# A GNN layer on one NeuronCore: in steps with picks, ScalarE normalises three of a block's four tiles and VectorE one

## The reference

```python
h = relu(layernorm(x))                 # x: 50000 x 128, no scale or shift
xx = resmlp(h, MLP 0)                  # for all nodes
xs, xp, xd = resmlp(h, MLP 1, 2, 3)[dst]       # for 12500 edges
s = xx + segment_sum((rbf @ w_rs) * xs, src)
p, d = segment sums of (rbf @ w_rp) * xp * attr3 and of (rbf @ w_rd) * xd * attr5
y = s + inner products of the halves of p @ w_pp and of d @ w_pd
out = x + resmlp(y, MLP 4)

def resmlp(x, w1, b1, w2, b2, wout):
    h = x + silu(silu(x) @ w1 + b1) @ w2 + b2
    return silu(h) @ wout
```

## Time and profile before

| | |
|---|---|
| median of 3 runs | 1262.18 us (1259.76 to 1266.66) |
| the profiled execution | 1264.56 us |
| its span, first to last instruction | 1262.7 us |
| mean granted TensorE clock | 0.963 |
| busy: PE, ACT, DVE, POOL | 1135.0, 758.2, 660.6, 456.9 us |
| HBM read and written | 93.01 and 96.30 MB |

### The profile page before, as it was taken

One profiled execution on the slowest core, in us unless ns is written; L12 is line 12 of the kernel. 1 busy time (PEld: TensorE's weight loads), 2 busy tenths in 40 slices (PEclk: granted clock), 3 DMA queues, 4 the chain that ended last, 5 costly groups with the idle time before them and its releaser, 6 DMA issues.

```text
span 1262.7 us, 23295 instructions
## 1 busy us (share of the span) xinstructions
PE 1135.0 (90%) x6835; PEld 766.0 (61%) x6835; DVE 660.6 (52%) x2466; ACT 758.2 (60%) x1425; POOL 456.9 (36%) x423
## 2 busy tenths in 40 slices
PE   2778998797989856999999999999977999999998
PEld 1555665474656533666666666666744666666665
DVE  9866876695778303565556555655541222222222
ACT  2357878656877833555655565556524666666665
POOL 3055666015565531456555655565340000000000
PEclk9889999898999978999999999999988999999999
DMA  7166667735766430233333333333435888788876
GB/s 223 67 213 199 224 213 224 253 129 162 232 217 211 165 89 11 46 57 46 54 55 57 47 54 55 55 49 52 83 55 170 250 263 263 247 266 258 256 257 206
DMA packets 162765, 190.56 MB, mean 151 GB/s; under 512 B 57956, under 2 KB 82444, under 8 KB 162413
## 3 DMA queue, kind: packets, MB, share of 16 engines
q1 hardware_dynamic: 124636, 144.39, 38.4%
q0 software_dynamic: 23920, 19.29, 9.7%
q10 hardware_dynamic: 14112, 25.70, 5.3%
HBM read 93.01 MB, written 96.30 MB: 150 GB/s over the span
## 4 chain that ended last, share of the span: by engine, by line
PE 77%; DVE 11%; issue 7%; DMA 2%; ACT 1%; another core or an unknown queue 1%; SPq 0%; POOL 0%; ACTq 0%; POOLq 0%; DVEq 0%
PE bank L976 7%; PE quad L964 7%; PE bank L1489 5%; PE quad L968 5%; PE bank L1499 5%; PE bank L811 4%; PE quad L795 4%; PE bank L1563 4%; PE bank L1531 3%; DVE onehot L589 3%; PE bank L1564 3%; PE quad L804 3%; PE quad L956 3%; PE quad L780 2%; DVE stat L484 2%
## 5 line engine op out<-in xcount | busy, mean ns | idle before, releaser
L1164 POOL DMA_INDIRECT node_sums<-rowout,row_i x98 | 155.0, 1582 | 199.6 <-ACT rowout L1426 177.1
L900 DVE TENSOR_TENSOR rowout<-bank,xin 128x512 f32<-128x512 f32 x98 | 67.8, 692 | 242.0 <-PE bank L976 242.0
L811 PEld LDWEIGHTS bank<-wo_sb,s 128*128 128x128 f32 x784 | 102.8, 194 | 64.9 <-issue 64.9
L431 POOL DMA_INDIRECT edges_by_src<-pay,rank_i x98 | 96.2, 981 | 111.5 <-DVE rank_i L619 50.6
L431 POOL DMA_INDIRECT edges_by_low<-pay,rank_i x98 | 96.6, 986 | 99.3 <-DVE rank_i L619 42.2
L976 PEld LDWEIGHTS bank<-wo_sb,s 128*128 128x128 f32 x784 | 102.8, 191 | 47.8 <-issue 47.8
L1197 DVE SCALAR_TENSOR_TENSOR h<-bank,b_sb,hT 128x512 f32<-128x512 f32 (+1 forms) x75 | 55.5, 740 | 122.2 <-PE bank L1499 122.2
L484 DVE BATCH_NORM_STATS2 stat<-xin 128x6 f32<-128x128 f32 x392 | 105.4, 284 | 21.9 <-DMA xin<-in_x_dram 21.9
L811 PE MATMUL bank<-wo_sb,s 128*128 128x128 f32 x784 | 106.0, 279 | 11.0 <-issue 9.0
L72 POOL DMA_INDIRECT yin<-node_h,er x98 | 94.9, 968 | 53.8 <-issue 29.3
L709 ACT ACTIVATE xn<-xin,nbias,rnorm 128x128 f32<-128x128 f32 x210 | 101.8, 492 | 14.3 <-DVE nbias L535 14.3
(11 more groups left out here) (193 smaller groups left out, 2376.1 us busy)
## 6 DMA issues: line engine op xcount, KB each, us to landing
xin<-in_x_dram SPq DMA_DIRECT2D x196, 256.0 KB, 3.9
node_h<-xn SPq DMA_DIRECT2D x98, 256.0 KB
node_sums<-rowout SPq DMA_DIRECT2D x98, 256.0 KB
yin<-node_sums SPq DMA_DIRECT2D x98, 256.0 KB, 4.0
out_dram<-rowout ACTq DMA_DIRECT2D x98, 256.0 KB, 3.8
border_sums_by_tile<-border_sums SPq DMA_DIRECT2D x24, 256.0 KB, 2.1
pay<-edges_by_low POOLq DMA_DIRECT2D x1, 2058.0 KB, 10.7
edges_by_low<-pay,rank_i POOLq DMA_INDIRECT x98
```

The source lines that it names most:

```text
L431: nc.gpsimd.indirect_dma_start(out=ps.dram, out_offset=bass.IndirectOffsetOnAxis(ap=rank_i[:, t:t + 1], axis=0), in_=pay[:, t, :], in_offs ...
L811: last = nc.tensor.matmul(BANK_O[:, j * P:(j + 1) * P], s3[:, (k - 3) % 3, j * P:(j + 1) * P], wo_sb[:, m, :], start=True, stop=True)
L1164: nc.gpsimd.indirect_dma_start(out=ysum, out_offset=bass.IndirectOffsetOnAxis(ap=row_i[:, t % 2, j:j + 1], axis=0), in_=urow[:, t % 2, j, ...
```

## The change

In steps with picks `by_scalar` gives 3 in place of 2: tiles 1, 2 and 3 are ACT's (tiles 1 and 2 ahead of L733, tile 3 behind it), and DVE's subtraction and rectification take tile 0 alone. The steps at the start of a pass (4) and the steps without picks (2) stay. No semaphore is added or taken away; the waits for `nrm_v`, `nrm_a` and the old store of the slot move with the tiles.

```diff
             def by_scalar(b):
 
                 k = max(b - 1, 0)
-                return TB if any(ps.onehots <= k <= ps.onehots + T // OH for ps in passes) else TB // 2
+                if any(ps.onehots <= k <= ps.onehots + T // OH for ps in passes):
+                    return TB
+                return 3 if picks_at(k) else TB // 2
```

## The result

| | before | after |
|---|---|---|
| median of 15 runs each, one after the other | 1261.82 us (1258.41 to 1266.66) | 1267.36 us (1264.62 to 1269.64) |
| ratio | | 1.0043, 95% interval 1.0032 to 1.0054 |
| span of the profiled execution | 1262.7 us | 1267.8 us |

The kernel is 5.5 us slower, 0.43%, against 5.6 us forecast. The interval of the ratio leaves out 1, so the loss is real, though small.

What follows compares the result with a forecast made beforehand. PE was taken to set the pace, waiting for ACT's last normalisation after a disturbance. 4.3 us from 11 disturbed B steps plus 1.3 from 15 undisturbed made 5.6 us, 0.44%, so 1268 us; range 1256 to 1275 (8 in 10).

Steps and rivals of the forecast that it cites:

- disturbance: About every second or third step: ACT idles 1.5 to 2.1 us, matmul completion reaching it late, and PE runs dry.
- A steps: 28 steps with a chunk's first four picks, 3.84 us each; ACT's waiting there covers the extra 0.39 us: cost nothing.
- A steps past 3.84 us: Sign in the profile after that the prediction would be wrong: A steps growing longer than 3.84 us.
- B steps without a disturbance: 15 steps with a chunk's last three picks: 12 lose 0.06 us, three 0.20, sum 1.3 us; 3.11 for 3.05 us.
- The three with a lag: Three undisturbed B steps, step 32 first, where ACT came in slightly late: 0.20 us late each.
- B steps with a disturbance: 13 steps with a chunk's last three picks: 11 listed blocks lose 0.39 us each, 4.3 us; two lose nothing.
- The next stage's loads near 460: SP's first loads of the next stage were to start near 460 in place of 454.20, the first stage's loss staying lost.
- Free steps: Steps without picks, still two and two: way back after a disturbance no longer than now; ACT's lateness goes into 2.11 us waiting.
- DVE's relief: DVE's subtraction and rectification 0.28 us less a step, 15.7 us busy time in all; taken as worth nothing on the path.
- the rival with the other sign: Rival that DVE was the bound, each step it sets gaining 0.28 us: faster, 1255.2 us with 45 such steps; chance 0.13.
- ACT becomes the bound in every B step: Rival: ACT's list 3.28 us against PE's 3.05, all 28 B steps cost 0.39: 10.9 us, 1273.1; chance 0.17.
- The disturbances hide it: Rival: late completions come at fixed times, so only undisturbed B steps' 1.3 us stays: 1263.5 us; chance 0.20.

Runs made afterwards that it cites:

- VectorE's part alone: Kernel before, with VectorE normalising one tile in steps with picks, ScalarE still two and tile 1 left out: 1267.25 against 1265.76 us, ratio 1.0007.
- ScalarE's part alone: Kernel before, with ScalarE also normalising tile 1 into an unread tile in steps with picks, VectorE still two: 1270.53 against 1265.76 us, ratio 1.0039.
- the A steps alone: Changed kernel with three tiles on ScalarE in A steps only, against the kernel before: 1266.17 against 1265.76 us, ratio 1.0002.
- the chip without disturbances: Changed kernel, unaltered, against the kernel before on a chip where the latter takes 1194 us: 1195.86 against 1194.00 us, ratio 1.0015.
- the opposite change: Kernel before with ScalarE one tile, VectorE three in B and free steps, two and two in A: 1261.83 against 1264.70 us, ratio 0.9979.

## Why the prediction was right

- *PE sets the pace, ACT's last normalisation is what it waits for behind a disturbance, and in no step of the two stretches VectorE.* Shown: VectorE's part alone 1.0007, ScalarE's part alone 1.0039 of 1.0043. (The 28 A and 28 B steps that the prediction counts are those of the two whole passes; the two stretches of the earlier trace rows hold fewer.)
- *A steps cost nothing.* Shown by the A steps alone (1.0002), and by the 0.46 us of wait that went. The prediction also named A steps past 3.84 us as a sign of being wrong, and two came out so (11 and 63, above). They are longer by a disturbance that fell there and not by the added operation, which stands ahead of the idle time; what such a shift is worth by itself no run tells.
- *B steps without a disturbance cost 0.06 us.* They cost 0.05: 3.10 for 3.05 in all traces. The three with a lag, put at 0.20, take 3.10 as well, where they took 3.05 to 3.07. On the chip without disturbances 28 x 0.05 is 1.4 us, and measured by the ratio were 1.8 (0.4 to 3.2). In its traces the step behind a B step is some 0.03 us longer too: 0.66 us for the 8 B steps between blocks 18 and 38 and 0.97 for the 12 between 58 and 87, so 0.08 for each.
- *B steps with a disturbance cost 0.39 us.* True of block 26, 0.38 us by its idle time. As a list of eleven blocks it is not what happened: once steps are longer the disturbances fall otherwise. In the profile after the B steps 20 and 30 are 1.18 and 1.10 us longer and the free steps 18 and 28 0.57 and 0.54 shorter. From block 18 to 38 the sum is 1.97 us, where the prediction's terms for them (four blocks at 0.39, four B steps at 0.06 to 0.20) give 1.9; from 63 to 87 it is 3.7 against 2.5; and from block 4 to 18 the profile after took 2.0 us less. By the medians the part that needs disturbances is 5.5 less 1.8, 3.7 us, against 4.3 forecast.
- *The next stage's loads near 460.* They came at 457.76: the first stage of that pair lost 3.6 us. The 5.5 us is a difference of medians.
- *Free steps keep their length.* Wrong in the single step: some are half a us shorter, which the longer B steps more than make up.
- *DVE's relief and the rival with the other sign.* This rival fell by VectorE's part alone (1.0007), as did "ACT becomes the bound in every B step": its 0.39 us in each would be 10.9 us, and the chip without disturbances shows 0.05, or 0.08 with the step behind.
- *The disturbances hide it.* This rival also fell for the change (ACT's idle time stayed near 40 us, and the loss is four times its 1.3 us), but when the work was taken away, in the opposite change, most of the gain did not come: 2.9 us of up to 9.8. So the full price of 0.39 us behind each disturbance held for adding work and not for taking it away.

That the sum came out within 0.1 us of the measured one is partly luck: one execution differs from the next by more, and the positions of the disturbances were taken from a single one. The prediction held that about 0.5% can be told from no change; with 15 executions of each kernel it was 0.11% either way.

What stays open: why the matmuls' completion reaches ScalarE late on one chip while GpSimd scatters, and not on two others, and whether the spacing of the scatters matters there.

## What to carry to other kernels

When work moves between engines, find for each kind of step which engine's last instruction releases the bound one, and by how much; a move costs the instruction's full share of a back-to-back row (0.39 us here, not its recorded 0.49) where that gap is zero, the overrun where it is small, and nothing where the engine waits. Do it per kind of step, not by busy shares: here VectorE was at 76% and ScalarE at 78%, both under PE, and in these stretches only one of them was waited for. The releaser named by a view is checked against the block or tile that the waiting instruction needs.

## What the runs showed of the hardware

- The same kernel took 1262 to 1266 us where it was first measured and on the chip of the first eight runs, and 1194 on two others. Most of the difference is in the first stage: up to the last block's transposes 443.1 us and 384.2, which is 58.9 of the 71.3 us between the spans (1262.7 and 1191.4). From 98 to 199 us ACT has ten idle times of 0.7 to 2.1 us in the one trace, and none in the other.
- Two of these idle times, looked at in the trace's semaphore records, end when several of PE's signals come at once, though its matmuls are recorded as done at different times before. In the kernel before, the output matmuls, the transposes and the first matmul ended by their records at 147.43, 147.86 and 148.72 us, and their semaphores were counted up at 148.87, 148.93 and 148.97; ACT's copy started at 148.89. At 160.54 to 160.70 four came so, for matmuls that ended at 158.46, 158.90, 159.76 and 160.62; the copy started at 160.56.
- Where they occur, they are there while GpSimd issues indirect transfers and gone when it does not: from block 58 to 87 it is 112.8 and 97.5 us. With the transfers, and on a chip without disturbances, it is 97.5 too.
- In a row of back-to-back work, a 128x128 activation with scale and bias takes 0.39 us of ScalarE's time though the profile gives it 0.49 us; 0.38 us was what PE's idle time grew by where nothing covered it (block 26).
- The two operations of VectorE took 0.42 us at 128x256, 0.29 and 0.28 at 128x128, and 0.55 at 128x384.
